# The Q and K evictions go from VectorE to ScalarE, and the output stores from ScalarE's queue to GpSimd's

## The reference

```python
x = x + attn(layernorm(x), Wq, Wk, Wv, Wo)
x = x + ffn(layernorm(x), w_fc, w_proj)

def attn(x, Wq, Wk, Wv, Wo):
    q = einsum('bsd,ed->bse', x, Wq)
    k = einsum('bsd,ed->bse', x, Wk)
    v = einsum('bsd,ed->bse', x, Wv)
    kvt = cumsum(k * v, axis=-2) * (sqrt(D) / seq)
    return einsum('bse,fe->bsf', q * kvt, Wo)

def bitlinear(x, w):                    # x: layer norm, then rounded to a grid by its largest value
    gamma = mean(abs(w))
    w_hat = sign(round(w / (gamma + EPS))) * gamma
    return einsum('bsd,od->bso', quantised(layer_norm(x)), w_hat)

def ffn(x, w_fc, w_proj):               # 2048 -> 8192 -> 2048
    return bitlinear(gelu(bitlinear(x, w_fc)), w_proj)
```

## Time and profile before

| | value |
|---|---|
| median of 5 runs | 8678.32 us |
| the profiled execution, its own time | 8709.47 us |
| its span on the slowest core (core 7) | 8707.9 us |
| spans of the 8 cores | 8623.7 to 8707.9 us |
| PE busy | 6086.4 us, 70% |
| DVE busy | 1822.7 us, 21% |
| ACT busy | 1256.1 us, 14% |
| POOL busy | 516.9 us, 6% |
| PE's idle time ahead of the matmuls of E, put down to a weight load | 404.7 us in 8 times, one of them 397.7 us |
| PE's idle time ahead of the matmuls of F, put down to a weight load | 226.1 us in 232 times |

### The profile page before, as it was taken

The page is one execution under the profiler, slowest core; times in us unless marked ns, Lnnn a source line. Parts: engine busy times, 40 slices in busy tenths (PEclk is TensorE's granted clock), DMA queues, the critical chain, the costliest instruction groups (busy, mean ns, idle before and its releaser), DMA issues.

```text
span 8707.9 us, 84763 instructions; the slowest of 8 cores (8623.7 to 8707.9 us)
## 1 busy us (share of the span) xinstructions
PE 6086.4 (70%) x30984; PEld 2889.8 (33%) x30984; DVE 1822.7 (21%) x2893; ACT 1256.1 (14%) x1217; POOL 516.9 (6%) x916
## 2 busy tenths in 40 slices
PE   2600020058888888888888888887978797969797
PEld 1200010024344343433343334433434343434343
DVE  1101110111222222222222123212221222122212
ACT  0146535630001000001000100110011001000100
POOL 0001100100000000000000000000000000100010
PEclk9855565579999999999999999999989898989899
DMA  8978847876544564356435652565356534753475
GB/s 140 194 246 222 211 167 239 216 245 253 211 164 165 220 232 176 140 211 258 184 123 216 259 195 107 220 261 205 126 193 271 203 126 184 297 196 117 173 271 203
DMA packets 260452, 1750.51 MB, mean 201 GB/s; under 512 B 22353, under 2 KB 104402, under 8 KB 104402
## 3 DMA queue, kind: packets, MB, share of 16 engines
q0 software_dynamic: 194816, 1140.91, 37.9%
q1 hardware_dynamic: 60626, 570.62, 18.8%
q10 hardware_dynamic: 4608, 33.56, 1.0%
HBM read 1174.57 MB, written 100.66 MB: 146 GB/s over the span
## 4 chain that ended last, share of the span: by engine, by line
PE 56%; DMA 26%; issue 6%; DVE 6%; ACT 5%; DVEq 0%; ACTq 0%; POOLq 0%; SPq 0%; POOL 0%
PE pa L596 20%; PE pa L682 14%; PE pa L438 14%; DMA wpj<-wpj_b 11%; PE pa L532 5%; DMA h<-wfct 3%; DMA wfc_b<-h 2%; DMA h<-wpjt 2%; DMA wpj_b<-h 2%; PE pt L359 2%; ACT h L316 2%; ACT h L274 1%; DMA wk_b<-wkt 1%; DMA wv_b<-wvt 1%; DMA wq_b<-wqt 1%
## 5 line engine op out<-in xcount | busy, mean ns | idle before, releaser
L682 PE MATMUL pa<-wpj,hqT 128*128 128x512 bf16 x8192 | 1884.4, 387 | 330.7 <-DMA wpj<-wpj_b 226.1
L596 PE MATMUL pa<-wat,xnT 128*128 128x512 bf16 x8192 | 1782.2, 380 | 413.8 <-DMA wat<-wfc_b 404.7
L438 PE MATMUL pa<-wat,xnT 128*128 128x512 bf16 x6144 | 1341.3, 382 | 133.9 <-DMA wat<-wv_b 48.9
L596 PEld LDWEIGHTS pa<-wat,xnT 128*128 128x128 bf16 x8192 | 802.3, 98 | 1390.6 <-issue 436.4
L682 PEld LDWEIGHTS pa<-wpj,hqT 128*128 128x128 bf16 x8192 | 783.2, 99 | 1351.5 <-issue 534.3
L438 PEld LDWEIGHTS pa<-wat,xnT 128*128 128x128 bf16 x6144 | 604.4, 98 | 867.9 <-issue 153.1
L665 DVE COPY hqT<-pt 128x1024 bf16<-128x1024 bf16 x512 | 330.0, 685 | 1814.1 <-PE pt L656 1813.6
L614 DVE BATCH_NORM_STATS2 stH<-h 128x6 f32<-128x512 bf16 x512 | 331.1, 685 | 1576.7 <-ACT h L606 1576.7
L606 ACT ACTIVATE h<-pa 128x512 bf16<-128x512 f32 x512 | 305.9, 598 | 1402.4 <-PE pa L596 1402.2
L656 PE MATMUL pt<-cid,h 128*128 128x128 bf16 x4096 | 285.1, 224 | 283.3 <-DVE h L636 283.3
L359 PE MATMUL pt<-cid,xn 128*128 128x128 bf16 x1024 | 119.4, 309 | 516.6 <-ACT xn L415 278.9
(11 more groups left out here) (67 smaller groups left out, 2290.5 us busy)
## 6 DMA issues: line engine op xcount, KB each, us to landing
wat<-wfc_b POOLq DMA_DIRECT2D x256, 2048.0 KB, 7.7
wpj<-wpj_b POOLq DMA_DIRECT2D x512, 1024.0 KB, 4.7
h<-wfct SPq DMA_DIRECT2D x128, 1024.0 KB, 6.8
h<-wpjt SPq DMA_DIRECT2D x128, 1024.0 KB, 6.2
wat<-wk_b SPq DMA_DIRECT2D x32, 2048.0 KB, 14.2
wat<-wv_b SPq DMA_DIRECT2D x32, 2048.0 KB, 8.2
wat<-wq_b SPq DMA_DIRECT2D x32, 2048.0 KB, 8.8
wat<-wo_b SPq DMA_DIRECT2D x32, 2048.0 KB, 8.0
```

Of the source, the lines that this page charges most:

```text
L438: tm = emit("pe", lambda e, _sl=sl, _b=b, _d=d, _bk=bank: e.matmul(pa[_bk][:, :], xnT[:, _b * D + _d * 128:_b * D + (_d + 1) * 128], wat_v ...
L596: tm = emit("pe", lambda e, _sl=sl, _gb=gb, _d=d, _bk=bank: e.matmul(pa[_bk][:, :], xqT[:, _gb * D + _d * 128:_gb * D + (_d + 1) * 128], w ...
L682: tok = emit("pe", lambda e, _lb=lb, _gp=gp, _dd=dd, _w=wsl, _d4=dd4, _ep=ep, _dp=dprime, _bk=bank: e.matmul(pa[_bk][:, :], hqT[:, (_lb * ...
```

## The change

Two things change. The copies of K and of Q out of PSUM are issued on ACT with its own copy operation instead of on DVE; the multiplication for V stays on DVE. And the stores of the finished rows are issued from POOL's list instead of ACT's, with the wait for the last stores at the end of the program moved along with them. Sizes, buffers, waits and the other instructions stay as they are.

```diff
                         if cname == "k":
-                            emit("ve", lambda e, _b=b, _e=e4, _bk=bank: e.tensor_copy(
+                            emit("act", lambda e, _b=b, _e=e4, _bk=bank: e.copy(
                                 qv[:, _b * D + _e * 512:_b * D + (_e + 1) * 512],
                                 pa[_bk][:, :]),
                                 rd=[("pa", bank)], wr=[("qv", b, e4)], deps=[tm])
...
                         else:
-                            t_q[(b, e4)] = emit("ve", lambda e, _b=b, _e=e4, _bk=bank: e.tensor_copy(
+                            t_q[(b, e4)] = emit("act", lambda e, _b=b, _e=e4, _bk=bank: e.copy(
...
             for lb in range(NBF):
                 gb = sub * NBF + lb
-                dma("act", s_out[gb % 2], out[(i * NBA + gb) * 128:(i * NBA + gb + 1) * 128, :],
+                dma("pool", s_out[gb % 2], out[(i * NBA + gb) * 128:(i * NBA + gb + 1) * 128, :],
                     xsl(i, gb), rd=[("x", gb, ee) for ee in range(NED)],
                     wr=[("xf", gb)], deps=x2_toks[lb])
...
         for so in s_out:
             if so.count:
-                bd.raw_wait("act", (so, so.count))
+                bd.raw_wait("pool", (so, so.count))
```

## The result

The changed kernel was timed at 9140.84 us, the median of 6 runs (8833.54 to 9530.49), against 8681.56 us of 10 runs of the kernel before. The ratio of the comparable runs is 1.0244, with a 95% interval of 1.0178 to 1.0311. Repeated beside the experiments it was 1.0157 (1.0081 to 1.0233). The forecast was 8819 us, a ratio of 1.016 to 8678. The direction held. On the 8678 of the forecast, 1.0244 is 8890 us, 2 us above the range of 8742 to 8888, and 1.0157 is 8814 us, inside it.

What follows compares the result with a forecast made beforehand. PE was taken to set the pace, with lateness at phase borders deciding. Borders 131 us plus first tile 10 gave 141 over 8709.5, 8850, or 8819 us on the runs' median of 8678; range 8742 to 8888.

Steps and rivals of the forecast that it cites:

- The stall at E1: Border F0 to E1: POOL's stores delay E1's first weight load, PE starts 14.4 us later, 2 of it for x.
- The clock: E1's first matmuls: PE loses clock after idling 14 to 16 us, 2.2 us a border, between 0 and 2.4.
- The sum of both: Eight borders F0 to E1: 16.6 us each, 131 us since the last loads no x; bounds 74 and 164.
- The border between two tiles: F1 to the next tile, 7 borders: x for block 2 waits for its store but has 8 us cover; cost nothing.
- The evictions: Copies of K and Q on ACT, phase B: hidden behind PE either way; steady cost and gain zero.
- The first tile: ACT's first sum over the feed-forward matrix starts 23 us later behind Q's evictions; net cost 10 us, between 3 and 23.
- The range: Whole kernel: 8742 to 8888 us, from bounds 8755 to 8865 plus some 15 us either side for run spread.
- The loads didn't pass the stores: Rival at E1: loads get past the stores, leaving only the first tile's 10 us, 8688 us; chance 5%.
- Freeing ACT of its stores: Rival at the 7 tile borders: ACT no longer held by its stores gains 37 us, giving 8651 us; chance 3%.
- The stall didn't go on beyond the first load: Rival at E1: loads two and three also late, 10 us more a border, 80 in all, 8899 us; chance 7%.

Runs made afterwards that it cites:

- the small stores: Changed kernel, but each of the two stores after F0 moves 64 KB instead of 1 MB: ratio 1.012, 8754.2 us against 8646.8 at full clock.
- E0: Not a run: the first half of phase E in a tile, ahead of F0; in the first tile of the kernel before it starts at 1810 us.
- the four slots: Kernel before with evictions of K and Q on ACT and F's weight loads through four 1 MB slots instead of two: ratio 0.9881.
- the transpositions: Version of the four slots, with F's next group's transpositions and DVE copies between this group's matmul halves: 8313.4 us against 8640.5 at full clock.

## Why the prediction was wrong, and where it was right

**The stall at E1: right.** Forecast 12.4 us for issue and bytes and 2 for x, 14.4 us a border. Measured at full clock: 15.4 us of idle time less the 1.7 of before, 13.7; 14.1 at the border shown (15.57 less 1.50). The parts hold too. In the sum the stores' bytes make the difference between 12.4 and 9.2 us, 3.2; the small stores show 3.5. Without x the sum says 12.4, and the last border shows 14.60 less 1.50, 13.1. x was put at 2 us; from issue to PE's start the first load took 12.1 us with x and 11.4 without (medians of four cores at full clock), 0.7 more, and 9.6 against 7.9 with the small stores (eight cores), 1.6 more, at most 3.4 on any core. In the changed kernel a load of x took 16.4 us to land. The Trainium skill (DMA: Bandwidth & Descriptors, Queues, rings and completion order) has each engine take turns between queue rows by packet; read as an even split of the rate, which would be 4.5 us, the traces disagree with it here. A packet isn't the same size on both sides: by the DMA view the two loads of x have 288 packets for 2.10 MB, and two weight loads before had 289 for 4.21 MB. By turns of whole packets x would take half the load's bytes, an estimate of 2.5 us from these counts, which is nearer to what was measured.

**The clock: right.** Forecast 2.2 us a border. The windows show 2.2 us at one, and E's matmuls on core 6 take 1795.6 us against 1780 to 1782 at full clock without the stall, 14 us or 1.8 a border.

**The sum of both: right.** 8 x (13.7 + 1.8) = 124 us; the stores alone measured 123, the change 128.5; forecast 131. That all four lie within 8 us is partly luck, since dies of one kernel at full clock differ by 16 to 52 us.

**The border between two tiles: right.** Forecast nothing. On core 6 of the repeated run the stores land 5.0 us and x 6.4 us after issue (5.3 and 6.3 in the earlier trace rows), x is issued at 3270.85 and DVE first needs it at 3284.61, and DVE waits for x once in the whole program, in the first tile, as before.

**The evictions: right.** Forecast zero, measured 3 us at full clock with an interval for the ratio that holds 1.

**The first tile: wrong in size.** The sums did start late, at 373 to 394 us on the cores of the repeated run against 354 to 367 before. But they end no later: 650 us on the mean of the cores in both runs of the changed kernel and 656 with the evictions alone, against 654 before and 652 with the stores alone. E0 starts at 1788 and 1795 us in the two runs of the changed kernel and at 1810 before, but also at 1799 with the stores alone, which leave the first tile as it was, so that difference is scatter. The term was put at 10 us with a floor of 3; it is 0 within a scatter of some 5. What was wrong is that the sum let 7 of the 23 us come back, where all of them did. On the changed kernel's core 5 the conversion that ran while ACT was busy with evictions took 20.4 us instead of the 39.6 of the earlier trace rows:

```profile
363.50 1.10 POOL L115 DMA_DIRECT2D wo_b<-wot  x1 [49.80 <-DMA wo_b<-wot]
383.93 1.10 POOL L115 DMA_DIRECT2D wo_b<-wot  x1 [19.32 <-DMA wo_b<-wot]
```

The last conversion is issued at 425.89, against 444.38 on the same core before, and its traffic beside the chunks ends that much earlier. From 354 to 377 us the engines move less on this core than before, 160 against 236 GB/s, and from 450 to 500 us more, 267 against 220; from 354 to 645 us it is 251 against 252. ACT, busy 26 of the 50 us from 500 to 550, was not what bound the stretch. Why the sum gave 7 us where the traces give the whole isn't settled further. Without this term the forecast would have been 8809, so it didn't cause the miss.

**The range: wrong, and this is the step that failed.** The term that was mis-sized is the 15 us on either side "for the spread of the runs (8654 to 8685 for four of five)". It left out the fifth of these runs, 9311.7, and with it what a lower granted clock costs. At full clock the first measurement's 8770.2 us is 1.0142 times the 8647.0 us of the kernel before, taken on the experiments' chip; the measured 1.0244 is about 1% more, some 90 us, where the range allowed 15. The traces show these as PE's own time: 6287.4 us busy at a mean clock of 0.839, 6102.8 at 0.861, in the same program. Where both dies were near full clock the changed kernel took 8791.03 and 8833.54 us, inside the range. The mechanism, its place and its size at full clock were as forecast. Whether the stall at E1 itself brings the lower clock on more often is left open; no run separates that from chance.

**The rivals.** The loads didn't pass the stores. Freeing ACT of its stores gained nothing: between the tiles of the earlier trace rows DVE waits 0.40 us for ACT's root before and after. The stall didn't go on beyond the first load: on core 6 each border has one idle time put down to wat.

## What to carry to other kernels

Before moving a DMA to another engine's list, look at what stands behind it there: a store waits for the last result of a phase, and a prefetch for the next phase often stands right behind. Here the busy shares said that POOL had room, and what counted was 10 us of lead in its list, which another order of three loads and two stores gave back. Size a late load as issue time, plus the bytes ahead of it, plus its own; and where one wait is removed, read what is late next before counting the gain, as the four slots and then the transpositions show.

## What the runs showed of the hardware

A copy of 128x512 float32 from PSUM to bf16 takes 585 to 586 ns on ACT and 692 on DVE. Loads of x on SP's queue issued into three 2 MB weight loads on POOL's took 14.5 us to land with small stores ahead and 16.4 with full ones, against 6.3 between two tiles, where no weight load of POOL's stands beside them, while the first weight load was held up by 0.7 us with full stores and 1.6 with small ones (medians; at most 3.4): the two queues did not share the bytes evenly. After about 15 us of idle time PE was granted 0.76 of its clock over the next 9.5 us, and 1.00, the upper level, over the 9.5 after that; after 1.50 us of idle time before, it was granted 1.00 from the start.
